# Row broadcasts by transfers instead of PE transposes, and one mask tile for two layers, in a four-layer graph network

## The reference, cut to what matters

```
x = layernorm(x + L0(x, adj))     # graph attention with additive scores
x = layernorm(x + L1(x, adj))     # graph attention with bilinear scores, ELU
x = layernorm(x + L2(x, adj))     # four-head attention, masked by adj or the diagonal
x = layernorm(x + L3(x, adj))     # relational convolution with a gate

# L0
Wh = x @ W.T;  s1 = Wh @ a1;  s2 = Wh @ a2
e  = leaky_relu(s1[:, None] + s2[None, :], 0.2);  e = where(adj == 0, -inf, e)
out = softmax(e) @ Wh

# L2, per head
scores = where(adj | eye, q @ k.T * scale, lowest);  out = relu((softmax(scores) @ v) @ Wo + bo)
```

## Time and profile before

| what | value |
|---|---|
| median of 3 runs | 496.18 us (496.12 to 496.77) |
| the profiled execution | 496.9 us, its span 495.0 us |
| busy: PE, ACT, DVE, POOL | 468.4, 428.0, 410.8, 370.6 us |
| mean granted PE clock | 0.988 of full |
| transfers | 26.93 MB, 18.4% of the 16 DMA engines' time for the kernel's queue |
| bytes from and to HBM | 17.63 MB read, 8.39 MB written |

### The profile page before, as it was taken

One profiled execution on the slowest core, in us unless ns is written; L12 is line 12 of the kernel. 1 busy time (PEld: TensorE's weight loads), 2 busy tenths in 40 slices (PEclk: granted clock), 3 DMA queues, 4 the chain that ended last, 5 costly groups with the idle time before them and its releaser, 6 DMA issues. The chain is left out here.

```text
span 495.0 us, 13988 instructions
## 1 busy us (share of the span) xinstructions
PE 468.4 (95%) x3872; PEld 402.3 (81%) x3872; DVE 410.8 (83%) x1605; ACT 428.0 (86%) x1261; POOL 370.6 (75%) x736
## 2 busy tenths in 40 slices
PE   6968999999999999999999999999999999999793
PEld 5756778988888888988888888888888888877572
DVE  5657898998888998898888988898898989876653
ACT  3558999999999999999999999999999999988750
POOL 1365576788888888888888888888888888986523
PEclk9989999999999999999999999999999999999997
DMA  7211111122112221222112221221123100000011
GB/s 219 74 44 44 44 54 52 40 63 66 40 48 66 66 66 54 54 66 63 36 56 66 65 60 51 66 65 43 45 66 87 34 23 13 23 24 23 22 45 44
DMA packets 40222, 26.93 MB, mean 54 GB/s; under 512 B 2641, under 2 KB 39889, under 8 KB 40146
## 3 DMA queue, kind: packets, MB, share of 16 engines
q1 hardware_dynamic: 40146, 26.03, 18.4%
...
HBM read 17.63 MB, written 8.39 MB: 53 GB/s over the span
## 5 line engine op out<-in xcount | busy, mean ns | idle before, releaser
L1211 POOL TENSOR_SCALAR x<-y,minus_mean,rstd 128x128 f32<-128x128 f32 x244 | 144.8, 601 | 6.8 <-issue 5.1
L788 ACT ACTIVATE p<-p,nmax 128x256 f32<-128x256 f32 x256 | 128.5, 530 | 0.4 <-DVE nmax L981 0.4
L981 DVE CUSTOM_DVE_ANT_0 p<-ps,neg 128x256 f32<-128x256 f32 x256 | 90.7, 420 | 2.3 <-PE ps L564 2.3
L1193 POOL TENSOR_TENSOR rstd<-ve,minus_half 128x2 f32<-128x2 f32 x128 | 91.1, 712 | 0.0
L575 PE MATMUL ps<-ident,p 128*128 128x128 f32 x512 | 78.0, 275 | 4.1 <-DVE nmax L981 3.4
L1186 POOL TENSOR_SCALAR ve<-stats 128x2 f32<-128x2 f32 x128 | 24.6, 192 | 72.3 <-DVE stats L896 64.9
L797 ACT COPY p2T<-ps 128x512 f32<-128x512 f32 x128 | 75.2, 590 | 1.3 <-PE ps L575 0.5
L575 PEld LDWEIGHTS ps<-ident,p 128*128 128x128 f32 x512 | 61.3, 143 | 9.3 <-DVE nmax L981 4.0
L788 ACT ACTIVATION_READ_ACCUMULATOR p<-p,nmax 128x1 f32 x256 | 56.1, 219 | 0.0
L896 DVE BATCH_NORM_STATS2 stats<-y 128x6 f32<-128x256 f32 x128 | 54.1, 423 | 1.5
L1175 POOL TENSOR_TENSOR relu<-relu,neg 128x512 f32<-128x512 f32 x32 | 37.1, 1161 | 21.1 <-ACT relu L757 21.1
(11 more groups left out here) (130 smaller groups left out, 1210.3 us busy)
## 6 DMA issues: line engine op xcount, KB each, us to landing
adj_in<-in_adj_dram SPq DMA_DIRECT2D x32, 256.0 KB, 3.0
xT<-in_xT_dram SPq DMA_DIRECT2D x32, 128.0 KB, 2.1
x_in<-in_x_dram SPq DMA_DIRECT2D x32, 128.0 KB, 2.1
x_aside<-x SPq DMA_DIRECT2D x32, 128.0 KB, 2.1
out_dram<-x SPq DMA_DIRECT2D x32, 128.0 KB, 2.9
...
l_w<-in_l_w_dram SPq DMA_DIRECT2D x1, 256.0 KB
...
```

Of the source, the lines that this page charges most:

```text
L788: last = nc.scalar.activation(p2(n)[:, k, a, :], p2(n)[:, k, a, :], ACT.Exp, bias=nmax2(n)[:, k, a:a + 1], scale=-1.0, accum_out=sum2(n)[: ...
L981: last = nc.vector.tensor_tensor_reduce(p2(n)[:, k, a, :], bank("sc2", n, a)[:, k * N:(k + 1) * N], neg2(n)[:, k, :], -1.0, HIGHEST, ALU.a ...
L1193: nc.gpsimd.tensor_tensor(rstd[layer](n), ve[layer](n), minus_half[:, :], ALU.pow)\
L1211: last = nc.gpsimd.tensor_scalar(dst[:, k, 0:D], y_t[layer](n)[:, k, :], minus_mean[layer](n)[:, k:k + 1], rstd[layer](n)[:, k:k + 1], ALU ...
```

## The change

- For graphs 3 and up the s2 row is made by two transfers: `s2_out` writes the columns s2 and 0.2 s2 of `xw0` to memory, 8 bytes for a node, and `s2_in` reads the 2 KB back to all 128 partitions. `proj0` gets a third extra weight column for 0.2 s2. `e0` reads both rows from that tile, in which they alternate. The first three graphs (`PE_ROWS`) still use PE and ACT.
- The reciprocal sums are turned as they are, 128 x 8 to 8 x 128, ACT copies 8 x 128, and two transfers (`rs_in`) broadcast each row to its head's 32 partitions. `rs_rep` goes.
- Layer 2's mask is made in place in `neg0`, which then waits for layer 0's reader `m0`, and only the two diagonal blocks are multiplied. `neg0` has 7 buffers instead of 3, `neg2` (6) goes.
- Two pairs of POOL's semaphores become one each.
- `PLAN` is a new table for all engines.

```diff
 RING = {
-    "adj": 5, "x": 3, "xT0": 2, "neg0": 3, "neg1": 3, "neg2": 6, "eq1": 7, "xw0": 3, "s2row": 2, "p0": 2, "p0T": 2,
+    "adj": 5, "x": 3, "xT0": 2, "neg0": 7, "neg1": 3, "eq1": 7, "xw0": 4, "s2row": 3, "p0": 2, "p0T": 2,
...
+    **{step: (0, PE_ROWS) for step in ("s2_rows", "c_s2")},
+    **{step: (PE_ROWS, 0) for step in ("s2_out", "s2_in")},
...
+        diagonal = lambda n: neg0(n).rearrange("p t (a b) -> p (t a) b", b=P)[:, ::T + 1, :]
...
+            def rs_in(n):
+                sp.wait_ge(sem("rs_sb"), n + 1)
+                free(sp, "rs_row", n, "onT_sb")
+                for k in range(T):
+                    sp.dma_start(rs_row(n)[:, k * P:(k + 1) * P],
+                                 rs_turned(n)[k * HEADS:(k + 1) * HEADS].rearrange("h (a i) -> h a i", a=1)
+                                 .broadcast_to((HEADS, DK, P))).then_inc(sem(f"rs_in{n % RING['rs_row']}"), 16)
+
+            def s2_out(n):
+                sp.wait_ge(sem("wh_sb"), n + 1)
+                sp.dma_start(s2_dram[n].rearrange("(t p) c -> p t c", p=P), xw0(n)[:, :, 1:3])\
+                    .then_inc(sem(f"s2_out{n % 2}"), 16)
+
+            def s2_in(n):
+                sp.wait_ge(sem(f"s2_out{n % 2}"), 16 * ((n - PE_ROWS) // 2) + 16)
+                free(sp, "s2row", n, "e0_ready")
+                sp.dma_start(s2row(n).rearrange("p j c -> p (j c)"),
+                             s2_dram[n].rearrange("(a j) c -> a (j c)", a=1).broadcast_to((P, 2 * N)))\
+                    .then_inc(sem(f"s2_in{n % RING['s2row']}"), 16)
...
             def rs_rows(n):
                 o = bank("rs_rows", n)
                 bank_free(pe, "rs_rows", n)
-                pe.wait_ge(sem("rs_rep_ready"), n + 1)
-                for k in range(T):
-                    last = pe.transpose(o[:, k * P:(k + 1) * P], rs_rep(n)[:, k, :], ident[:, :])
-                last.then_inc(sem("rs_ps"), 1)
+                pe.wait_ge(sem("rsum2_ready"), n + 1)
+                pe.transpose(o[0:T * HEADS, 0:P], rsum2(n).rearrange("p t h -> p (t h)"), ident[:, :])\
+                    .then_inc(sem("rs_ps"), 1)
...
-                nc.scalar.copy(rs_row(n), bank("rs_rows", n)[:, 0:N]).then_inc(sem("rs_sb"), 1)
+                if n >= RING["rs_row"]:
+                    act.wait_ge(sem(f"rs_in{n % RING['rs_row']}"), 16 * T * (n // RING["rs_row"]))
+                rows = slice(0, T * HEADS)
+                nc.scalar.copy(rs_turned(n)[rows, :], bank("rs_rows", n)[rows, 0:P]).then_inc(sem("rs_sb"), 1)
...
             def e0(n):
-                dve.wait_ge(sem("s2_sb"), n + 1)
+                if n < PE_ROWS:
+                    dve.wait_ge(sem("s2_sb"), n + 1)
+                    row = bank("s2_rows", n)[:, 0:N]
+                else:
+                    dve.wait_ge(sem(f"s2_in{n % RING['s2row']}"), 16 * ((n - PE_ROWS) // RING["s2row"]) + 16)
+                    row = s2row(n)[:, :, 0]
                 free(dve, "p0", n, "pT_ps0")
                 for k in range(T):
-                    last = nc.vector.scalar_tensor_tensor(out=p0(n)[:, k, :], in0=bank("s2_rows", n)[:, 0:N],
-                                                              scalar=xw0(n)[:, k, 0:1], in1=s2row(n),
-                                                              op0=ALU.add, op1=ALU.max)
+                    last = nc.vector.scalar_tensor_tensor(out=p0(n)[:, k, :], in0=row, scalar=xw0(n)[:, k, 0:1],
+                                                          in1=s2row(n)[:, :, 1], op0=ALU.add, op1=ALU.max)
...
             def neg2_(n):
-                pool.wait_ge(sem("masks_ready"), n + 1)
-                free(pool, "neg2", n, "e2b_ready")
-                nc.gpsimd.tensor_tensor(neg2(n), neg0(n), not_eye[:, :, :], ALU.mult).then_inc(sem("neg2_ready"), 1)
+                pool.wait_ge(sem("m0_ready"), n + 1)
+                nc.gpsimd.tensor_tensor(diagonal(n), diagonal(n), not_eye[:, :, :], ALU.mult).then_inc(sem("neg2_ready"), 1)
...
-    "sync": [("ld_xT", 6707), ("ld_adj", 7906), ("ld_w", 8043), ("ld_x", 8602), ("aside", 16291), ("store", 19013)],
+    "sync": [("ld_xT", 7696), ("ld_w", 7941), ("s2_out", 8199), ("s2_in", 9000), ("ld_adj", 9574), ("ld_x", 10290),
+        ("rs_in", 14953), ("aside", 16550), ("store", 20067)],
```

More of the change, by code:

```diff
@@ L62 @@
 AT_END = 3
+PE_ROWS = 3
 GRAPHS = {
@@ L355, in _ @@
             sp.dma_start(first_w[:, :], t["first_w"]).then_inc(sem("w0_loaded"), 16)
-            run("sync", {"ld_adj": ld_adj, "ld_xT": ld_xT, "ld_x": ld_x, "ld_w": ld_w, "aside": aside, "store": store})
+            run("sync", {"ld_adj": ld_adj, "ld_xT": ld_xT, "ld_x": ld_x, "ld_w": ld_w, "rs_in": rs_in, "s2_out": s2_out, "s2_in": s2_in, "aside": aside, "store": store})
             for s in range(RING["x4"]):
@@ L389, in setup @@
                 pe.wait_ge(sem("w0_loaded"), 16)
-                pe.matmul(ps[:, 0, 0:2], first_w[:, W0], first_w[:, 0:2], start=True, stop=True)\
+                pe.matmul(ps[:, 0, 0:3], first_w[:, W0], first_w[:, 0:3], start=True, stop=True)\
                     .then_inc(sem("setup_pe"), 1)
@@ L434, in flag @@
                 pe.wait_ge(sem("excess_ready"), 2)
-                pe.matmul(o[0:1, 0:1], excess[:, :], xw0_all[:, 0, 0, D + 2:D + 3], start=True, stop=True)\
+                pe.matmul(o[0:1, 0:1], excess[:, :], xw0_all[:, 0, 0, D + 3:D + 4], start=True, stop=True)\
                     .then_inc(sem("excess_ps"), 1)
@@ L473, in proj0 @@
                 for k in range(T):
-                    last = pe.matmul(o[:, k * (D + 2):(k + 1) * (D + 2)], xT0(n)[:, k * P:(k + 1) * P], w0_w[:, :],
+                    last = pe.matmul(o[:, k * (D + 3):(k + 1) * (D + 3)], xT0(n)[:, k * P:(k + 1) * P], w0_w[:, :],
                                      start=True, stop=True)
```

67 lines of the change are left out of this document (31 added, 36 removed), and 34 rows, old and new, of the table PLAN.

## The result

| | before | after |
|---|---|---|
| median of the runs | 496.48 us (496.12 to 497.08) | 579.17 us (576.40 to 581.01) |
| span of the profiled execution | 495.0 us | 576.6 us |
| first scores, last scores, end (starts of qkT; span) | 39.22, 464.99, 495.0 | 43.60, 537.43, 576.6 |

The ratio is 1.1659 with an interval of [1.161, 1.1709]: a sixth slower, where 486.9 was forecast. The 81.6 us of span lie in three places: 4.4 in the filling, 68.1 between the first and the last scores (493.83 against 425.77) and 9.2 in the emptying (39.2 against 30.0). The filling is the time up to the first scores, the emptying the time from the start of the last scores on.

A forecast was written before the change was run, and what follows sets the result against it. PE's queue was taken as the bound, 14.00 us a graph. From 496.9 us, 5.9 + 0.6 + 0.9 + 0.6 + 1.8 - 0.5 = 9.3 gave 487.6, less 0.7 for the median 486.9; range 482.5 to 492.5.

The forecast's parts named there:

- part 4: SP's queue: the new transfers fit with nothing waiting in the middle; only the end loses, 0.5 us.
- The landings: New transfers' times from nearby rows: 2.1 us for 128 KB, 3.0 for 256 KB; s2_out bounded by 2.1 and 5.
- rival D: SP's queue: a late transfer costs each microsecond past the slack once per graph; around 500 if 0.5 over; chance 0.05.
- The end: Last graph: nothing covers rs_in before onT2, so 0 to 0.9 us lost, taken as 0.5.
- Part 1: PE's queue: two s2 transposes fewer save 0.22 us a graph, 5.9 us over 27 graphs.
- rival B: Middle stays at 14.0 us, paced by a loop through relu, POOL's add, e1 and exp1: 493.4 us; chance 0.11.
- rival C: DVE: e0, both tensors in SBUF, is caught behind POOL, 1.24 us more a graph: 511 us; chance 0.06.
- Part 2: PE: one 8-row transpose replaces two for the reciprocal rows, saving 0.01 to 0.11 us a graph; taken 0.02, 0.6 us.
- the optimistic end: PE: by record count alone, the 8-row transpose saves 0.11 us a graph, 3.5 us over 32.
- The rule on tiling mode: PE: changing tiling mode drains the engine, about 0.09 us a change, keeping the 8-row transpose's saving at the low end.
- Part 3: POOL and DVE: halved mask work is worth nothing; e0 changes by -0.07 to +0.09 us each, hidden.
- Part 5: Filling: the new order gains 0.9, 0.6 and 1.8 us, first scores at 37 to 38 us instead of 39.22.

The follow-up runs named there:

- e0: Not a run: a DVE instruction of the kernel, twice a graph, that reads the s2 row; changed to read it from SBUF instead of PSUM, mean 556 ns after.
- e2: The changed kernel with the reciprocal rows made by POOL, PE and ACT as before, the s2 rows still by transfers: 502.57 us.
- e11: e2 plus two broadcasts of rs_in's shape at its place, from a constant tile to one that nothing reads, without the wait: 502.27 us.
- e10: e2 plus only SP's wait for the copied rows at rs_in's place, transferring nothing there: 503.47 us.
- e14: The changed kernel with only ld_adj, ld_xT and s2_in moved ahead of rs_in in SP's queue: 503.17 us.
- e16: e14 with the reciprocal rows made by POOL, PE and ACT as in e2: 496.44 us.
- e7: The kernel before's table with s2 transfers and the mask in place, reciprocal rows by PE, proj0 and its copy a graph earlier: 499.44 us.
- e12: e7 with e0 alone moved in DVE's order, to just ahead of onT2: 498.29 us.
- e13: e7 with proj0 put back to its place in the kernel before and e0 a round later, for graph 3 and up: 494.62 us.
- e8: The kernel before in its own order with only the mask made in place and the semaphores joined: 497.53 us.
- e3: The changed kernel with s2 and reciprocal rows both made by PE again, keeping the mask in place and the new table: 509.07 us.

## Why the prediction was wrong

**The step that failed** is in part 4: "each needed some microseconds later. So 5 + 3 us fit and nothing waits in the middle". I checked the distances for the new transfers (s2_in to e0 and rs_in to onT2, "about half" a round each, 0.52 and 0.72 by the table), and only that from rs_in held: onT2 waited for rs_in once, 3.4 us at the end, while e0 waited 27.9 us for `s2row`, since s2_in is the transfer right behind rs_in. I did not work the distances out for the old loads that now queue behind rs_in's wait. ld_adj stands 0.13 rounds ahead of masks and ld_xT 0.01 ahead of proj0. Without rs_in such a table does no harm, since SP runs ahead of the engines until a buffer is missing (from 60 us on the loads are waited for 0.4 us in all in e2 and 0.2 in e11). With it SP is held to PE's pace in every round, and the nominal distance becomes the real one: masks waited 48.1 us for `adj_in`. The wait alone still leaves time for this (e10); with the slow issues and landings of the transfers on top the loop is longer than a round. e14 changes these places alone and gives back 76 of 83 us, which shows that the short distances are what costs in the presence of both.

**The landings** were the term mis-sized: 2.1 and 3.0 us from the earlier trace rows, measured 5.3 to 6.6 in the changed kernel; 7.62 us of issues from rs_in to ld_adj instead of some 3. "DMA engines at a fifth of their time" was no argument against rival D: what is issued behind rs_in was held up with the share at 0.20 (549 to 550 us).

**Rival D** named this mechanism with the words "SP stands behind rs_in so that ld_adj comes late", at 0.05 and an excess of 0.5 us. The excess was 2.2 us a round on average (68.1 in 31), 2.8 in the round shown: the mechanism was there and its price was about a quarter of the real one.

**The end** was to lose 0 to 0.9 us and lost 9. rs_in took 6.82 us, not 2.1 to 3.0, and I had left out the clock: in the changed kernel it is 0.50 from 556 to 576 us, behind the wait for this transfer (e14 against e16: 38.8 and 29.8).

**Part 1**, 0.22 us a round, was right in PE's queue and wrong as a gain. e7 had a round of 14.00 with two transposes fewer: rival B's picture, PE's saving given back as a wait for the bank that e1 frees (0.35 us in 24 rounds, 8.5 in all), caused by e0's meeting POOL (rival C's cause, 0.90 us a graph where it put 1.24). With e0 out of the way 0.12 to 0.22 come through (e12, e13). On the new table e0 is out of the way and the round is 14.00 all the same (e2, e16), probably by masks' meeting POOL, which no part of the prediction had.

**Part 2** was wrong in its choice. proj0 to the 8-row transpose is 0.45 (204.74 to 205.19), its step to the scores 0.20, 0.65 in all where proj0 to the scores (0.54) and the pair (0.22) took 0.76: no change of shape is paid on the way in, and 0.11 a graph is saved, the optimistic end. The rule on tiling mode that I leaned on isn't borne out for this entry; whether an 8-row transpose counts as a change of mode at all no run tells.

**Part 3** held: mask and POOL are worth nothing (e8); `neg2` fell from 1163 to 667 ns. That e0 changes by at most 0.09 us held only where POOL has nothing large beside it (475 ns in e2 and e13, 876 in e7).

**Part 5** was wrong: first scores at 37 to 38 us were forecast. They came at 43.60, and at 39.45 in e14, where the loads are in time, against 39.22 before. The new order of the filling gains nothing.

Still open is why two issues behind a broadcast of 4 rows take 2.2 to 2.5 us each and those behind one-row broadcasts don't, how much of e3's 11 us the s2 row's places cost, and whether masks beside rmask1 is what keeps the new table's round at 14.0.
